# Values of two key tiles in one visit, six exponential slots, values stored at 17 columns a head

## The reference, cut to what matters

```python
x = x + _L0_xattn_ref(_layernorm(x), ctx_1024, ctx_1024, ...)
x = x + _L0_ffn_ref(_layernorm(x), ...)        # attention of 16 heads, gates, projection
x = x + _L1_xattn_ref(_layernorm(x), ctx_1024, ...)
...
scores = jnp.einsum('bhqd,bhkd->bhqk', q, k) / scale
attn = jax.nn.softmax(scores, axis=-1)
ctx = jnp.einsum('bhqk,bhkd->bhqd', attn, v)
```

## Time and profile before

| what | us |
|---|---|
| median of 3 runs | 4612.67 (4611.46 to 4613.87) |
| the profiled execution, its own time | 4616.98 |
| span of the profiled execution | 4615.2 |
| PE busy in the span | 4301.1 |
| DVE busy in the span | 3017.3 |
| ACT busy in the span | 2512.8 |
| first and last visit to the values (L741) start at | 93.8 and 1794.4 |

### The profile page before, as it was taken

How to read it: one execution, slowest core, us unless ns; L and a number is a source line. 1 busy time by engine, 2 the same in 40 slices (tenths; PEclk the granted TensorE clock), 3 DMA queues, 4 the chain that set the end, 5 groups by cost and what they waited for, 6 DMA issues and landing times. The chain is left out here.

```text
span 4615.2 us, 66833 instructions
## 1 busy us (share of the span) xinstructions
PE 4301.1 (93%) x23718; PEld 2388.0 (52%) x23752; DVE 3017.3 (65%) x7437; ACT 2512.8 (54%) x5643; POOL 804.6 (17%) x550
## 2 busy tenths in 40 slices
PE   6999999999999996778698999999999998999998
PEld 2333343433333332557444666666666665555555
DVE  5777777777777776957684776676766766334343
ACT  3666666656666665633364767767676775111111
POOL 2322444443322311522100000000000000000000
PEclk7999999999999998989798999999999999999999
DMA  7455345344345450010200101101101101000001
GB/s 147 74 74 85 66 65 83 53 67 62 68 70 84 69 72 19 1 37 14 92 1 31 32 26 31 36 26 31 32 25 36 31 26 71 0 0 0 0 0 37
DMA packets 182660, 204.66 MB, mean 44 GB/s; under 512 B 44491, under 2 KB 164939, under 8 KB 180694
## 3 DMA queue, kind: packets, MB, share of 16 engines
q1 hardware_dynamic: 182358, 200.72, 22.2%
HBM read 139.90 MB, written 60.78 MB: 43 GB/s over the span
## 5 line engine op out<-in xcount | busy, mean ns | idle before, releaser
L465 DVE TENSOR_REDUCE L0x_maxes<-L0x_ps_max 128x1 f32<-128x512 f32 x1536 | 989.6, 685 | 289.2 <-PE L0x_ps_max L730 286.9
L646 ACT ACTIVATE L0x_probs<-L0x_ps_sc 128x1024 f32<-128x1024 f32 x768 | 777.5, 1026 | 429.5 <-PE L0x_ps_sc L719 423.7
L730 PE MATMUL L0x_ps_max<-L0x_kstack,L0x_qstack 96*128 96x512 bf16 x1536 | 595.0, 388 | 27.6 <-DVE L0x_maxes L465 21.3
L2668 ACT ACTIVATE L3x_pexp<-L3x_ps,L3x_nmax 128x77 f32<-128x77 f32 (+2 forms) x1536 | 600.3, 432 | 0.0
L719 PE MATMUL L0x_ps_sc<-L0x_qstack,L0x_kstack 104*128 104x512 bf16 x1536 | 524.2, 382 | 10.9 <-ACT L0x_probs L646 6.4
L2550 DVE TENSOR_REDUCE L3x_nmax<-L3x_ps 128x2 f32<-128x154 f32 (+2 forms) x768 | 346.5, 507 | 242.2 <-PE L3x_ps L2781 239.8
L741 PE MATMUL L0x_ps_out<-L0x_probs,L0x_vpad 128*32 128x512 f32 x3072 | 413.1, 610 | 9.1 <-ACT L0x_heads_raw L654 8.6
L2676 ACT COPY L3x_pT<-L3x_ps 128x512 f32<-128x512 f32 x512 | 275.0, 593 | 226.7 <-PE L3x_ps L2789 226.3
L2189 ACT ACTIVATE L3f_act_g<-L3f_ps_gu 128x512 f32<-128x512 f32 x128 | 76.4, 597 | 564.6 <-PE L3f_ps_gu L2234 564.6
L730 PEld LDWEIGHTS L0x_ps_max<-L0x_kstack,L0x_qstack 96*128 96x128 bf16 x1536 | 149.1, 97 | 421.3 <-DVE L0x_maxes L465 322.9
L2566 DVE TENSOR_SCALAR L3x_pexp<-L3x_pexp,L3x_rsum 128x77 f32<-128x77 f32 (+2 forms) x1536 | 357.8, 306 | 6.8
(11 more groups left out here) (374 smaller groups left out, 6810.0 us busy)
## 6 DMA issues: line engine op xcount, KB each, us to landing
L0x_kstack<-parts_scratch SPq DMA_DIRECT2D x144, 256.0 KB, 9.2
L0x_qstack<-parts_scratch SPq DMA_DIRECT2D x144, 256.0 KB, 14.3
parts_scratch<-L0x_kparts SPq DMA_DIRECT2D x24, 768.0 KB, 3.6
parts_scratch<-L0x_qparts SPq DMA_DIRECT2D x24, 768.0 KB, 4.3
rel_scratch<-L3x_rel_e SPq DMA_DIRECT2D x32, 408.0 KB, 2.4
L3x_rel_d<-prob_scratch SPq DMA_DIRECT2D x32, 408.0 KB, 3.1
L0x_kv_in<-in_ctxT SPq DMA_DIRECT2D x16, 512.0 KB, 5.3
L3x_rel_t<-rel_scratch SPq DMA_DIRECT2D x32, 154.0 KB, 2.4
```

The lines of the kernel that those rows point to most:

```text
L465: V.tensor_reduce(maxes[:, t, head:head + 1], ps_max[:, unit % 2, :], AX.X, ALU.max).then_inc(max_taken, 1)
L646: nc.scalar.activation(probs[:, n % 4], ps_sc[:, 2 * (n % 2):2 * (n % 2) + 2, :], ACT.Exp, scale=HD ** -0.5).then_inc(probs_ready, 1)
L730: nc.tensor.matmul(ps_max[:, unit % 2, :], qstack[q.parity][0:ROWS, head, t * P:(t + 1) * P], kstack[q.parity][0:ROWS, head, :], start=Tru ...
L2668: i = nc.scalar.activation(pexp[:, n % 4, e, a:b], ps[:, SB + 2 * (n % 2) + e, a:b], ACT.Exp, bias=nmax[:, n % 4, s, e:e + 1], accum_out=s ...
```

## The change

A visit to the values now covers two key tiles (eight matmuls, 16 records) and is made every fourth step, at the end of the steps with n % 4 = 1, for the four steps up to n - 2. `probs` has six slots instead of four, and the exponentials of every fourth step wait for a visit. `vpad` holds 17 columns a head (16 values and one of ones) and 15 more at the end; the stationary operand still has 32 columns, the last 15 of which are now the next head's and are not used.

```diff
+    SLOTS = 6
+    PER = 4
...
-        vpad = [ph.sb(f"vpad{b}", [P, TILES, HEADS, 32], F32) for b in range(2)]
+        vpad = [ph.sb(f"vpad{b}", [P, TILES, HEADS * (HD + 1) + 15], F32) for b in range(2)]
...
-        probs = ph.sb("probs", [P, 4, 2, S], F32)
+        probs = ph.sb("probs", [P, SLOTS, 2, S], F32)
...
-                V.tensor_tensor(vpad[q.parity][:, 2 * half:2 * half + 2, :, 0:HD],
+                V.tensor_tensor(vpad[q.parity][:, 2 * half:2 * half + 2, 0:HEADS * (HD + 1)]
+                                .rearrange("p b (h e) -> p b h e", h=HEADS)[:, :, :, 0:HD],
...
-                if n % 2 == 0 and (q.later or n >= 4):
-                    act.wait_ge(probs_used, q.count(STEPS // 2, n // 2 - 1))
-                nc.scalar.activation(probs[:, n % 4], ps_sc[:, 2 * (n % 2):2 * (n % 2) + 2, :], ACT.Exp,
+                at = q.count(STEPS, n)
+                if at >= SLOTS and (at - SLOTS) % PER == 0:
+                    act.wait_ge(probs_used, (at - SLOTS) // PER + 1)
+                nc.scalar.activation(probs[:, at % SLOTS], ps_sc[:, 2 * (n % 2):2 * (n % 2) + 2, :], ACT.Exp,
...
-                act.wait_ge(probs_used, q.count(STEPS // 2, 4 * g + 4))
+                act.wait_ge(probs_used, q.count(STEPS // PER, 2 * g + 2))
...
-            def values(q, pairs, waited):
-
-                g, kt = pairs // 8, pairs % 8 // 2
+            def values(q, first, waited):
+
+                g = first // 8
                 if not waited:
-                    pe.wait_ge(probs_ready, q.count(STEPS, pairs + 2))
-                if kt == 0 and (g >= 1 or q.later):
+                    pe.wait_ge(probs_ready, q.count(STEPS, first + PER))
+                if first % 8 == 0 and (g >= 1 or q.later):
                     pe.wait_ge(out_taken, q.count(4, g))
-                for j in range(4):
-                    i = nc.tensor.matmul(ps_out[32 * j:32 * j + 32, :], vpad[q.parity][:, kt, 4 * g + j, :],
-                                         probs[:, (pairs + j // 2) % 4, j % 2, :], start=(kt == 0),
-                                         stop=(kt == TILES - 1), tile_position=(0, 32 * j))
+                for k in range(2):
+                    kt = first % 8 // 2 + k
+                    for j in range(4):
+                        head = 4 * g + j
+                        i = nc.tensor.matmul(ps_out[32 * j:32 * j + 32, :],
+                                             vpad[q.parity][:, kt, (HD + 1) * head:(HD + 1) * head + 32],
+                                             probs[:, q.count(STEPS, first + 2 * k + j // 2) % SLOTS, j % 2, :],
+                                             start=(kt == 0), stop=(kt == TILES - 1), tile_position=(0, 32 * j))
                 i.then_inc(probs_used, 1)
...
-                    if n % 2 == 1 and (q if n > 1 else q.plus(-1)).there:
-                        values(q if n > 1 else q.plus(-1), (n - 3) % STEPS, q.there)
+                    if n % PER == 1 and (q if n > 1 else q.plus(-1)).there:
+                        values(q if n > 1 else q.plus(-1), (n - 5) % STEPS, q.there)
```

## The result

The changed kernel takes 4641.65 us (median of 5 runs, 4635.14 to 4642.36), the kernel before 4612.67 (5 runs, 4609.73 to 4613.87). The ratio is 1.0058, with a 95% interval of 1.0047 to 1.0070: slower by about 27 to 29 us. The profiled execution has a span of 4639.9, 24.7 longer.

The account below looks back on a forecast made before the run. PE and DVE were taken to bound the stream in turns. Terms 17 + 5 - 4 + 3 - 1.5 = +19.5 us, rounded to +20 on 4612.67, gave 4633 us, range 4603 to 4656.

Parts of the forecast that it names:

- PE and DVE bound the stream in turns: Stream of attentions: a removed visit's worth depends on which engine ends last; `ps_max` banks hold matmuls despite PE near 97%.
- A visit taken away returns 0.2: PE's values visits: two cost 2.20 us, one double visit 2.00; 192 removed, 38 us if PE bounded every stretch.
- the ten items: Cross items 1 to 5 and 17 to 21: each 1.7 us longer, +17 us together.
- The stretches: Eight four-step stretches of a cross item: 13 to 25 shorter, the others longer; sum 69.45 to 71.1 us.
- Items 0 and 6 to 8: Items with fewer or other fills: 1.2 us longer each, +5 us together.
- Items 9 to 16: Mixture items, fills at steps 2 to 5 and 7 to 21: 0.5 us shorter each, -4 us together.
- The stall at the gates: Mixture items, steps 17 to 25: PE's 2.98 us idle behind a gate operation on DVE stays.
- The last two items and the double visit behind them: Almost no fills: some 8 plain stretches at 0.2, 0.9 for the last double visit, a `heads_raw` wait gone: +3 us.
- The start: Before the stream: smaller memsets, 2 x 1.80 to 2 x 1.01, and normalisation ending up to 1.6 us earlier: -1.5 us.
- The first (PE's pace decides, 4573): Rival: held matmuls are absorbed, 192 visits x 0.20 come off, 4573 us; half of it 4593; chance 0.14 together.
- The third (weights of the second tile not loaded ahead): Rival: each double visit's tile boundary costs 0.1 us, 19 us more, 4652; chance 0.10.
- The second, balance: Rival: losses counted 1 us an item too high, 4609, or mixture clock drop vanishes, 4625 and less; chance 0.20.

Follow-up runs that it names:

- the first and the second move: Changed kernel with DVE's statistics, moments and normalisation moved, in cross items to steps 5, 9, 13 (first, 4626.09 us) or 5, 5, 9 (second, 4621.99 us).
- the kernel with chosen visits: Changed kernel with double visits only in 61 of 192 stretches, ones shorter in its profile, single visits elsewhere: 4604.48 us, ratio 0.9981 to the kernel before.

## Why the prediction was right

**PE and DVE bound the stream in turns.** Shown: with DVE's load halved the change turns from +29 to -41, and the earlier trace rows's waits are those of the profile after.

**A visit taken away returns 0.2.** Entering costs 0.32 as taken, leaving 1.85 instead of 1.90. All passes were sized by the 0.45 between the two of a visit; of the four, the second still starts 0.45 after the first, but the third and the fourth 0.43 after theirs. That is 0.05 for each of 192, or 0.4 for a cross item, which lost 1.17 and not 1.7: the ten items gave 11.7 instead of 17. That these 0.05 are the whole reason is not shown, since the misses of the stretches run from -0.15 to +0.03.

**The stretches.** All eight have the sign that was forecast, the largest miss is 0.15. DVE idle went to 302.7, not some 290.

**The other terms.** Items 0 and 6 to 8 together: 6.0 (forecast 5). Items 9 to 16: -1.6 (forecast -4), scattered from -2.5 to +2.5. Up to step 17 the stretches of items 9 to 13 changed by +0.62, -0.34, +0.29 and -0.66, where +0.75, 0, +0.35 and -0.6 were forecast; the scatter lies in 21 to 25, with the clock. The stall at the gates stays, as forecast, and so does the half clock behind it:

```profile
1017.73 0.39 PE L734 MATMUL L0x_ps_max<-L0x_kstack,L0x_qstack 96*128 96x512 bf16 x1 [3.01 <-DVE L0x_maxes L467]
...
1018.55 3.29 PE L769 MATMUL L0x_ps_t<-L0x_wo_mixture,L0x_hT 128*128 128x256 f32 x8
```

The last two items and the double visit behind them: 2.9 (forecast 3). The start: the normalisation beside the shorter memsets took 3.07 instead of 4.57, and the first matmul came 1.3 earlier (12.26 instead of 13.52), much as forecast. But the second four matmuls of the k projection, 0.9 earlier still at 21.74, then took 3.78 where the same four at 22.64 took 1.98 before, and the visit at step 5 came at 97.5, 0.4 later. That is 2 us off the forecast, lost ahead of the first double visit. Nor is it tied to the change: the changed kernel with the first and the second move makes that visit at 95.5 and 97.5.

```profile
8.74 1.05 POOL L415 MEMSET L0x_vpad<- 128x1148 f32 x1
8.83 3.07 DVE L445 TENSOR_SCALAR L0x_xn<-x_res,L0x_mv,L0x_rstd 128x256 f32<-128x256 f32 x4 [1.41 <-POOL L0x_rstd L342]
```

The sum in the stream is 18.6 + 0.9 = 19.5 where 19.5 was forecast. That it agrees so well is luck: the 5 too much for the ten cross items was made up by the start, the mixture items and items 0 and 6 to 8. The measured 29 holds 5 more that no term had: 2.7 behind the last visit, nearly all of it where the clock falls, and 2.5 in an untouched sublayer. The other 4 are the profiled execution before, which was slower than its median.

**The rivals.** The first (PE's pace decides, 4573) needs DVE's holes not to hold PE. At half load the total comes near it (41 for its 38 and 1.5), though not stretch by stretch: 13 to 17 gives 0.88 and 9 to 13 loses 0.35. The third (weights of the second tile not loaded ahead) is out: the double visit lasts 1.92, under the bound of 2.1. The second, balance, did not occur, but the move of DVE's work reaches it. That ACT's slots cost nothing holds: no wait of the exponentials for a visit shows. Nor did `take_v` change: 0.69 at a step of 17 columns as at one of 32.

## What to carry to other kernels

A busy share of 97% does not say that an engine is the bound: look at the distances between the starts of its instructions, and at whether the other engine's buffers set them. Making a long chunk of PE work longer costs the engine that PE feeds a hole of the same size, unless its buffers (here two banks, 1.2 us of DVE's work) outlast the chunk or it has other work to put there; ask this for each stretch, since the removal pays in the stretch where the chunk stood and the price falls due in the one behind its new place. Where a merge pays only in some stretches, do it there; or move the starved engine's unrelated work to the steps of the holes. Here either took away the loss, and in the cross items the two together gave no more than the first alone (68.89).

## What was not expected of the hardware

In the mixture items the granted clock of TensorE falls to 1.2 GHz in one item and not in the next, with the same program: in the kernel with chosen visits the stretch 21 to 25 took 12.85 in two of the items 9 to 13, at a granted clock of 1.00, and 14.1 to 14.5 in the others, at 0.88. This spread of 1.3 to 1.7 an item is as large as most of the effects here, and it is why the items were compared stretch by stretch. And the fp32 passes of the four column groups are not evenly spaced: the second starts 0.45 after the first, the two of the next key tile 0.43 after theirs (1.92 for four passes against 1.06 for two, so 0.86 for two more). The boundary between the tiles costs nothing beyond that.
